# Two attention layers of a decoder: key tiles added up on GpSimd, projections in pieces, maxima three slots ahead

## The reference

```python
def _L1_attn_ref(x, w_q, w_k, w_v, w_o):          # x is layer-normalised
    q, k, v = x @ w_q.T, x @ w_k.T, x @ w_v.T     # 16 heads of 32
    scores = einsum('bhqd,bhkd->bhqk', q, k) / sqrt(32)
    return (softmax(scores) @ v) @ w_o.T
def _L1_xattn_ref(q, latent_kv, Wq, Wkv_expand, Wout):
    k, v = split(latent_kv @ Wkv_expand.T, 2)     # latent_kv has 128 columns
    scores = where(causal, (q @ Wq.T) k / sqrt(32), lowest)
    return (softmax(scores) @ v) @ Wout.T
x = x + _L1_attn_ref(layernorm(x), ...)
x = x + _L1_xattn_ref(layernorm(x), ctx_512, ...)
x = x + _L1_ffn_ref(layernorm(x), ...)            # "the network", which follows
```

## Time and profile before

| What | us |
|---|---|
| Median of three runs | 2957.02 |
| The profiled execution | 2967.87 |
| Its span | 2966.1 |
| Start of the self layer (its input is loaded) | 1494 |
| First scores with maxima (L440) | 1555.7 |
| Last sums (L463) | 2397.9 |
| First matmul of the network (L2691) | 2424.0 |

### The profile page before, as it was taken

The page is one execution under the profiler, slowest core; times in us unless marked ns, Lnnn a source line. Parts: engine busy times, 40 slices in busy tenths (PEclk is TensorE's granted clock), DMA queues, the critical chain, the costliest instruction groups (busy, mean ns, idle before and its releaser), DMA issues. The chain is left out here.

```text
span 2966.1 us, 34593 instructions
## 1 busy us (share of the span) xinstructions
PE 2490.3 (84%) x12822; PEld 1652.2 (56%) x12822; DVE 1781.1 (60%) x2772; ACT 1225.8 (41%) x1859; POOL 791.4 (27%) x1054
## 2 busy tenths in 40 slices
PE   5899999984344369889769999999999879999999
PEld 4554545421222248788645454545555548888887
DVE  3766666546799977777636655655565444444443
ACT  3343434335766725455314333443433223333332
POOL 2223232213566626878600000001211110000000
PEclk8999999986666679999879999999999889999999
DMA  3313132202222357999732323333533331101000
GB/s 108 77 44 86 44 86 47 68 19 94 85 94 90 111 186 221 268 255 268 188 95 65 93 72 78 91 97 94 128 88 94 115 125 67 43 1 43 1 29 15
DMA packets 177017, 287.09 MB, mean 97 GB/s; under 512 B 20769, under 2 KB 52385, under 8 KB 176866
## 3 DMA queue, kind: packets, MB, share of 16 engines
q1 hardware_dynamic: 159458, 249.73, 28.7%
q0 software_dynamic: 14336, 34.61, 5.4%
q10 hardware_dynamic: 3072, 0.79, 0.1%
HBM read 149.79 MB, written 58.98 MB: 70 GB/s over the span
## 5 line engine op out<-in xcount | busy, mean ns | idle before, releaser
L657 DVE TENSOR_REDUCE at_negmax<-at_ps 128x2 f32<-128x1024 f32 (+3 forms) x256 | 259.2, 1017 | 131.5 <-PE at_ps L420 66.6
L572 ACT ACTIVATE at_probs<-at_ps 128x1024 f32<-128x1024 f32 (+3 forms) x256 | 221.8, 866 | 265.3 <-PE at_ps L440 262.5
L1258 DVE TENSOR_REDUCE a_negmax<-a_ps 128x2 f32<-128x1024 f32 x128 | 155.2, 1217 | 137.4 <-PE a_ps L1011 136.8
L50 PE MATMUL ff_ps<-ff_xnT_hi,ff_s_hi 128*128 128x512 f32 x512 | 201.0, 393 | 5.1 <-DVE ff_xnT_lo L2782 5.1
L52 PE MATMUL ff_ps<-ff_xnT_hi,ff_s_lo 128*128 128x512 f32 x512 | 200.2, 391 | 0.0
L51 PE MATMUL ff_ps<-ff_xnT_lo,ff_s_hi 128*128 128x512 f32 x512 | 200.1, 391 | 0.0
L1842 ACT ACTIVATE gr_act_signs<-gr_signed,gr_test 128x512 bf16<-128x512 f32 x248 | 177.3, 717 | 25.6 <-POOL gr_test L2221 14.0
L1159 ACT ACTIVATE a_probs<-a_ps 128x1024 f32<-128x1024 f32 x128 | 130.9, 1024 | 137.8 <-PE a_ps L1029 137.3
L2812 DVE TENSOR_TENSOR ff_hid<-ff_hid,ff_ps 128x512 f32<-128x512 f32 x64 | 44.0, 688 | 238.8 <-ACT ff_hid L2757 238.8
L440 PE MATMUL at_ps<-at_qk 98*128 98x512 f32 (+3 forms) x512 | 171.7, 417 | 17.6 <-DMA at_qk<-at_mrow 10.8
L440 PEld LDWEIGHTS at_ps<-at_qk 98*128 98x128 f32 x512 | 83.1, 193 | 158.7 <-issue 89.9
(11 more groups left out here) (416 smaller groups left out, 6425.9 us busy)
## 6 DMA issues: line engine op xcount, KB each, us to landing
at_qk<-at_part SPq DMA_DIRECT2D x384, 128.0 KB, 2.3
first_gu<-in_L_ffn_w_gate_up_dram SPq DMA_DIRECT2D x32, 1024.0 KB, 6.2
a_qk<-a_part SPq DMA_DIRECT2D x192, 128.0 KB, 2.3
first_d<-in_L_ffn_w_down_dram SPq DMA_DIRECT2D x32, 512.0 KB, 7.8
gr_aside_raw<-in_L_ffn_W_dram SPq DMA_DIRECT2D x48, 256.0 KB, 3.3
w13T<-gr_aside_out SPq DMA_DIRECT2D x32, 256.0 KB, 3.2
shared_x<-x_after_cross SPq DMA_DIRECT2D x8, 1024.0 KB, 8.0
ff_slab<-w13T SPq DMA_DIRECT2D x14, 512.0 KB, 6.3
```

The lines of the kernel that those rows point to most:

```text
L50: pe.matmul(out, lh, rh, start=start, stop=False, skip_group_check=True)
L572: act.activation(probs[:, t % 2, 2 * w:2 * w + 2, lo:S], banks(("kq", g, s), lo), ACT.Exp, scale=SCALE).then_inc(free(("kq", g, s)), 1)
L657: dve.reduce_max(negmax[:, g % 2, :].rearrange("p (j t) -> p j t", t=NT)[:, 2 * w:2 * w + 2, t], banks(("qk", g, s), 0, width(g, t)), AX.X ...
L1258: dve.reduce_max(negmax[:, g % 2, :].rearrange("p (j t) -> p j t", t=NT)[:, 2 * w:2 * w + 2, t], banks(("qk", g, s)), AX.X, negate=True).t ...
```

## The change

*Sums.* The exponentials of a pair get a buffer of their own: five of them (`halves` and a third of `got`), three in turn for pair 0 and two for pair 1. GpSimd adds the second to fourth key tile of each pair onto the first (`fold`, six additions per step, at slots 2 to 7, 128 x 1024 numbers each in the self layer); the first of them waits until the first tile has been weighed. `add_up` runs once per group, in slot 1 of the next step, in a pair of banks that it takes in turn, and waits for all six additions. `weigh` stands at slots 2, 4, 6 and 0. An exponential waits for the addition and the weighing that free its buffer.

*Maxima ahead.* `scores_qk` and the reductions run three slots earlier (`ahead`); `turn_maxima` and both `maxima_rows` stand at slot 5 of the step before instead of at its end.

*Projections.* The 8 pieces of a projection (three matmuls each) stand in slots 1, 2, 3, 5, 6 and 7 (`PIECES`), with one bank, PROJ, which was that of the sums, for q and then for k; ScalarE and VectorE empty it at slot 4 and at the end of the step.

*Inputs.* The transposes stand at slot 0 of c = 1; the input is measured in step c = 3 of the batch before, and normalised on GpSimd, one tile each at slots 1 to 4 of c = 0.

*The network's second chunk* is loaded after the last store of the loop, since one of the five buffers lies in its place.

```diff
-        probs = sb("probs", [P, 2, QUAD, S])
+        halves = sb("halves", [P, 4, 2, S])
...
-        NUM, SUMS = 6, 7
+        NUM, PROJ = 6, 7
+        SHIFT, TURN, NORMALIZE = 3, 5, 6
+        PIECES = {1: (0,), 2: (1,), 3: (2, 3), 5: (4,), 6: (5,), 7: (6, 7)}
...
-        UNITS = {(1, 1): ("o", 0), (1, 4): ("o", 1), (1, 6): ("x", 0), (2, 3): ("v", 0), (3, 3): ("v", 1)}
+        UNITS = {(1, 1): ("o", 0), (1, 4): ("o", 1), (1, 0): ("x", 0), (2, 3): ("v", 0), (3, 3): ("v", 1)}
...
+        def ahead(g, s):
+            return divmod(PAIRS * (g + 1) + s + SHIFT, PAIRS)
...
+        def both_of(g, t, w):
+            i = ((0, 1, 2, 1)[t] - g) % 3 if w == 0 else 3 + (g + (t > 0)) % 2
+            return halves[:, i] if i < 4 else got[:, 2]
+
+        def probs_of(g, t, j):
+            return both_of(g, t, j // 2)[:, j % 2, :]
...
+                load_chunk(0)
+
+            def load_chunk(k):
+                sp.dma_start(ff_chunk(got, None, k)[:, 0:2, :], w13T.rearrange("(k p) (m e) -> k p m e", p=P, m=2)[k]).then_inc(ff_in, 16)
+                sp.dma_start(ff_chunk(got, None, k)[:, 2, :], w2_mixed.rearrange("(k p) d -> k p d", p=P)[k]).then_inc(ff_in, 16)
...
+            sp.wait_ge(sums_done, G)
+            sp.wait_ge(values_done, NT * G)
+            for k in range(1, FF_AHEAD):
+                load_chunk(k)
...
-            def add_up(g, t):
-                lo = first(g, t)
-                if t == 0 and g >= 1:
-                    pe.wait_ge(sums_out, g)
+            def add_up(g):
+                key = claim("s", g)
+                for w in range(2):
+                    pe.wait_ge(folded[w], (NT - 1) * (g + 1))
                 for j in range(QUAD):
-                    mm = pe.matmul(ps[j * HD:(j + 1) * HD, SUMS, lo:S], ones[:], probs[:, t % 2, j, lo:S],
-                                   start=t == 0, stop=t == NT - 1, skip_group_check=True)
+                    mm = pe.matmul(bank(key, 0)[j * HD:(j + 1) * HD, :], ones[:], probs_of(g, 0, j), start=True, stop=True, skip_group_check=True)
...
-            def project(g):
+            def project(g, piece):
                 c, b = g % NC, g // NC
-                wait_drained(pe, "xT", b, 1)
-                if cross(b):
-                    wait_drained(pe, "cT", b)
-                    wait_drained(pe, "w", 0)
-                    wait_drained(pe, "w", 1)
-                    if c >= 2:
-                        wait_drained(pe, "w", 2)
-                key = claim("p", g)
-                for i, (w, src, n) in enumerate(((wqT, xnT, NC), (cross_wkT, cT, 1) if cross(b) else (wkT, xnT, NC))):
-                    for dc in range(n):
-                        mm = split_mm(pe, bank(key, i), [p[:, dc, c * P:(c + 1) * P] for p in w], [p[:, dc, :] for p in src], dc == 0, dc == n - 1)
+                i, dc = piece // NC, piece % NC
...
+                    if 2 * g + i:
+                        pe.wait_ge(p_out, 2 * g + i)
...
+                mm = split_mm(pe, ps[:, PROJ, :], [p[:, dc, c * P:(c + 1) * P] for p in w], [p[:, dc, :] for p in src], dc == 0, dc == n - 1)
+                if dc == n - 1:
...
-                    if has(g + 1):
-                        scores_qk(g + 1, s)
-                    if s >= 2 and has(g):
-                        half(g, s - 2)
-                    if s < 2 and has(g - 1):
-                        half(g - 1, PAIRS - 2 + s)
+                    if has(ahead(g, s)[0]):
+                        scores_qk(*ahead(g, s))
+                    if s == TURN and has(g + 1):
+                        turn_maxima(g + 1)
+                    if s >= 2 and s % 2 == 0 and has(g):
+                        weigh(g, s // 2 - 1)
+                    if s == 0 and has(g - 1):
+                        weigh(g - 1, NT - 1)
+                    if s == 1 and has(g - 1):
+                        add_up(g - 1)
...
-                if has(g + 1):
-                    turn_maxima(g + 1)
-                if has(g + 3):
-                    project(g + 3)
+                    if has(g + 3):
+                        for piece in PIECES.get(s, ()):
+                            project(g + 3, piece)
...
-                if NT * g + t >= 2:
-                    act.wait_ge(sums_done, NT * g + t - 1)
-                act.activation(probs[:, t % 2, 2 * w:2 * w + 2, lo:S], banks(("kq", g, s), lo), ACT.Exp, scale=SCALE
+                if t == 0 and g:
+                    act.wait_ge(values_done, NT * g - (1, 0)[w])
+                    act.wait_ge(folded[w], (NT - 1) * g - (1, 0)[w])
+                if t == 1 and g:
+                    act.wait_ge(sums_done, g)
+                if t == 3 or (t, w) == (2, 1):
+                    old = t - 2 + w
+                    act.wait_ge(values_done, NT * g + old + 1)
+                    act.wait_ge(folded[w], (NT - 1) * g + old)
+                act.activation(both_of(g, t, w)[:, :, lo:S], banks(("kq", g, s), lo), ACT.Exp, scale=SCALE
...
+            def keep_projection(g, i):
+                if g and i == 0:
+                    act.wait_ge(stack_in[(g - 1) % STACKS], 16 * 3 * QUAD * ((g - 1) // STACKS + 1))
+                act.wait_ge(p_ready, 2 * g + i + 1)
+                act.copy(part[:, 1 + i, :], ps[:, PROJ, :]).then_inc(p_hi, 1)
...
-            def layernorm(b):
-                dve.wait_ge(rstd_done, b + 1)
-                for t in range(NT):
-                    dve.tensor_scalar(xs(b)[:, t, :], xs(b)[:, t, :], mv[:, t, 0:1], rstd[:, t:t + 1],
-                                      ALU.subtract, ALU.mult).then_inc(xn_done, 1)
...
+            def low_projection(g, i):
+                dve.wait_ge(p_hi, 2 * g + i + 1)
+                dve.tensor_tensor(part[:, 3 * i, :], ps[:, PROJ, :], part[:, 1 + i, :].bitcast(F32), ALU.subtract).then_inc(p_out, 1)
...
+            def fold(g, t, w):
+                lo = first(g, t)
+                if causal(g):
+                    pool.wait_ge(masked, PAIRS * (g - NC * B) + 2 * t + w + 1)
+                else:
+                    wait_drained(pool, "kq", g, 2 * t + w)
+                if t == 1:
+                    if not causal(g):
+                        wait_drained(pool, "kq", g, w)
+                    pool.wait_ge(values_done, NT * g + 1)
+                else:
+                    pool.wait_ge(folded[w], (NT - 1) * g + t - 1)
+                total, part_of = both_of(g, 0, w)[:, :, lo:S], both_of(g, t, w)[:, :, lo:S]
+                pool.tensor_tensor(total, total, part_of, ALU.add).then_inc(folded[w], 1)
...
+            def layernorm(b, t):
+                if t == 0:
+                    pool.wait_ge(rstd_done, b + 1)
+                pool.tensor_scalar(xs(b)[:, t, :], xs(b)[:, t, :], mv[:, t, 0:1], rstd[:, t:t + 1], ALU.subtract, ALU.mult).then_inc(xn_done, 1)
...
-                for s in range(PAIRS if has(g) and causal(g) else 0):
-                    mask_diagonal(g, s)
-                if has(g - 1):
-                    pool.wait_ge(rec_done, NT * g)
-                    if g - 1 >= NC:
-                        pool.wait_ge(y_ready, 2 * ((g - 1) // NC))
-                    pool.tensor_tensor(oT[:, (g - 1) % NC, :], weighed[:, 0, :], weighed[:, 1, :], ALU.mult).then_inc(o_done, 1)
-                if g % NC == 0 and 1 <= g // NC + 1 < ALL:
-                    rstds(g // NC + 1)
+                for s in range(PAIRS):
+                    if has(g) and causal(g):
+                        mask_diagonal(g, s)
+                    if has(g) and s >= 2:
+                        fold(g, s // 2, s % 2)
+                    if g % NC == 0 and 1 <= s < 1 + NT and 1 <= g // NC + 1 < ALL:
+                        layernorm(g // NC + 1, s - 1)
+                    if s == NORMALIZE and has(g - 1):
+                        normalize(g - 1)
```

99 lines of the change are left out of this document (55 added, 44 removed).

## The result

The changed kernel takes 2974.73 us (median of six runs, 2969.69 to 2986.30), the kernel before 2960.26 (six runs beside it): a ratio of 1.0057, with a 95% interval of 1.0033 to 1.0080. It is slower by some 15 us where 74 less were forecast. Its profiled execution has a span of 2970.6 us, 4.5 more than the one before.

A forecast was written before the change was run, and what follows sets the result against it. TensorE was taken to set the time, almost alone in the self layer. Self layer -53, cross layer -32, start +4 and network +7 gave -74 us, 2883 at the median (before: 2957); 8-in-10 range 2845 to 2925.

The forecast's parts named there:

- So they just fit, with nothing over: Self layer: GpSimd's six additions and normalising per group, 15.6 us, fit a bare group's 19.8 and end before the sums.
- the count of 11.7 us against some 17: Cross layer: GpSimd's additions, eight masks and normalising take 11.7 us per group, against a group of some 17.
- Masks behind the normalisings: Cross layer, first group of a batch: masks wait behind input normalisings, 1.3 us three times, 4 us lost.
- Normalising: Layer's input on GpSimd: 1.45 us per tile, at most 2.9; only late exponentials cost, 3 us; at 2.9, 30 us.
- The clock: Cross layer's end: TensorE ran at 0.70 of its clock for 45 us; fewer waits there gain 7 us.
- The sums in the self layer: Three of four quads of sums per group leave TensorE, 47.5 us saved.
- The end: Cross layer's last two groups: waits of 7.7 and 3.1 us become work, 11 us gained, 3 lost again.
- The start: First batch's start: nothing covers the normalisings and the turns of the single bank, 4 us net lost.
- the new wait for the rows of maxima: First score of each cross group: rows of maxima land 1.7 us late, 12 times, 20 us lost.
- GpSimd becomes the bound: Rival, chance 0.08: additions of 3.35 us and normalisings of 2.9 or more make GpSimd late, taking the whole gain: 2970.
- The cross layer gives nothing: Rival, chance 0.13: late stack transfers make waits of 3 to 4 us per group and lower TensorE's clock: 2916.
- GpSimd blocks VectorE: Rival, chance 0.04: VectorE's reciprocals wait half a GpSimd addition each, 4 x 1.2 us a group: 2907.

The follow-up runs named there:

- the normalisings in the gap: Changed kernel with all four normalisings of the layer's input on VectorE in slot 1 of a batch's first group, where GpSimd pauses: 2934 us, ratio 0.9906.
- masks first: Changed kernel with GpSimd making both masks of a key tile before that tile's two additions in the cross layer: 2955 us, ratio 0.9984.
- gap, early load, masks first: Changed kernel with the normalisings in the gap, the early load and masks first together: 2912 us, ratio 0.9823.
- narrow additions: Changed kernel with each of a group's six additions on 2 x 32 columns only, so the sums lack the rest: 2912 us, ratio 0.9848.
- gap, early load, masks first, narrow: The kernel of gap, early load, masks first with each addition on 2 x 32 columns only: 2895 us, ratio 0.9784.
- the two and the early load: Changed kernel with the normalisings in the gap, the cross layer's additions on VectorE one slot later, and the early load: 2936 us, ratio 0.9926.
- the run without masks: Changed kernel without the masks on the cross layer's diagonal blocks and the waits for them: 2947 us, ratio 0.9955.
- the early load: Changed kernel with the network's second chunk loaded ahead of the last two stores instead of behind them: 2970 us, ratio 1.0032.

## Why the prediction was wrong, point by point

**The step that failed** is "So they just fit, with nothing over", and for the cross layer the count of 11.7 us against some 17. Both compare GpSimd's busy time with the length of a group. What decides is which instruction stands behind which. It sets three prices wrong:

- *Masks behind the normalisings* were 4 us; the waits for masks are 31 us, because masks also stand behind additions, and in every group. The order alone gave 20 us back at the median, the normalisings in the gap 15 us of the cross layer.
- *Normalising*: 1.45 us taken, 2.08 measured, inside the bounds. The last addition was followed to the sums, where it is late by some 1 us per wait (8.8 us in the layer). The late exponential behind it, put at "about 0.7 us on a bank", costs up to 2.9 us at the scores, four times, and 1.1 more behind (14.8 us in the layer, where 3 were counted), with a low clock after it. By the stretches of the run with the gap the normalisings cost 39 us, where the upper bound of 2.9 us each had been put at 30.
- *The clock* was to gain 7 us in the cross layer. It cost about as much as the added waits. The stretch from group 16 to the last sums, by busy time and by the sum of TensorE's waits in the order of time:

| Kernel | stretch | waits | TensorE busy | granted clock |
|---|---|---|---|---|
| before (2221 matmuls) | 380.8 | 30.5 | 349.7 | 0.95 |
| changed (1831) | 399.1 | 52.2 | 345.9 | 0.88 |
| masks first (1831) | 375.7 | 43.0 | 331.6 | 0.92 |
| gap, early load, masks first (1830) | 374.3 | 38.9 | 334.3 | 0.91 |
| narrow additions (1831) | 363.8 | 34.7 | 328.3 | 0.94 |
| gap, early load, masks first, narrow (1831) | 356.4 | 30.5 | 324.8 | 0.95 |

The same 1831 matmuls take 324.8 us at 0.95 and 345.9 at 0.88, 21 us more, while the waits grew by 22 from the kernel before. At the old clock the sums that went were worth 349.7 - 324.8 = 25 us, for 28 in the forecast; in the changed kernel 4 of it are left. That the waits bring the clock down is argued and not shown: clock and waits go together over most of the table, and the rows above show a slow stretch behind a wait twice, but no run changed one without the other, and a run outside the table doesn't fit (the two and the early load: 40.5 us of waits, 353.8 busy, 0.86).

**Right terms.** The sums in the self layer: the stretch is 19.0 us shorter while TensorE's idle time in it rose from 14.0 to 37.9 us, so its busy time fell by 43, for 47.5. The addition's 2.38 us. The wait for the last maximum. The end: the last two groups before the last take 49.3 us for 58.3, 9 less (8 forecast), but that holds their share of the sums too, and the last group gives 6.4 back to masks. The start, 5.5 for 4, from the normalisings: it is 66.9 to 71.0 us in the runs with these on GpSimd and 60.5 to 63.1 in those without. The load behind the last store, 4.9 for 7, and its remedy 5.5.

**A wrong term that didn't decide:** the new wait for the rows of maxima, 20 us. It is 3.8 us in the cross layer. In the run without masks it is 10.7, so other waits may hide part of it; with narrow additions and all remedies it is 4.8, so the projections and scores of slots 5 to 7 cover most of it after all.

**The rivals.** "GpSimd becomes the bound", 0.08, comes nearest. Its place was right (first groups of a batch, masks waiting with it) and its point wrong: it was to decide from 3.3 us for an addition, and the loss came at 2.39 and 2.08. That its 2970 lies near the time is partly luck, since it had the sums 70 us late, which were 8.8 late in the self layer; exponentials, masks and the clock made up for it. "The cross layer gives nothing", for late stacks, had the effect (low clock behind waits of 1 to 5 us) with another cause. "GpSimd blocks VectorE" doesn't happen in the changed kernel, where VectorE's reciprocals and statistics keep their 0.94 and 0.64 us; the runs that put such an instruction there show it.

**The signs.** Those listed as right mostly came: no long wait at the turn, additions of 2.39 us, GpSimd busy 63% of the self layer, groups without units every 21.5 us, the network 7.2 us behind the last store (8 or more were asked). Of those listed as wrong only the waits at the sums came, just (8.8 us in four batches). None asked for masks or exponentials, where most of the loss was.

**What stays open.** With the additions narrow and the three remedies, the stage is 68.7 us shorter than before, for 92 that the forecast's terms give without the charges then gone (load 7, start 4, exponentials 3, masks 4). Of these 23 us, 11 are in the self layer and 12 in the cross layer. Their busy times tell where (columns as above; each time the kernel before, the changed one, and the one with narrow additions and all remedies, in the self layer and then from group 16 to the last sums):

```profile
1555.65:2017.12 461.47, 447.44 (x2254) 235.01 (x2254) 268.54 (x338) 183.33 (x210) 23.68 (x21) 1.00 0.33 84
...
1557.06:1999.52 442.46, 404.60 (x1875) 232.54 (x1876) 257.66 (x322) 181.90 (x210) 277.12 (x131) 0.98 0.34 87
...
1545.52:1961.30 415.78, 399.62 (x1876) 229.59 (x1876) 263.52 (x338) 182.21 (x210) 52.03 (x116) 0.99 0.36 93
```

```profile
2017.12:2397.93 380.81, 349.67 (x2220) 209.85 (x2221) 208.15 (x310) 134.08 (x205) 74.48 (x147) 0.95 0.36 97
...
1999.52:2398.63 399.11, 345.91 (x1830) 216.15 (x1831) 197.06 (x291) 137.17 (x206) 225.20 (x258) 0.88 0.34 90
...
1961.30:2317.74 356.44, 324.77 (x1831) 202.56 (x1831) 202.21 (x303) 135.98 (x206) 102.34 (x245) 0.95 0.38 101
```

In the self layer the sums' work went in full in the last of these, 47.8 us for 47.5, but TensorE's idle time (the stretch less its busy time) is 16 us for the 14 before: the 9 us of waits at the turn came back as other short ones, for banks and inputs. In the cross layer the idle time is the same, 32 us for 31, and the work fell by 25, where 28 of sums and 7 of clock were counted. What causes each of the short waits no run took apart. Nor is it settled why second groups of the self layer take 37.0 us at a clock of 1.00 in some runs and 38.6 at 0.96 in others, with the same program for that layer: in two that were compared the waits of TensorE are alike, the longest 1.0 us, and one has a stretch at the lower clock level behind them and the other has none.

## What to carry to other kernels

An idle engine has room for work only behind what it already does for others: before moving work there, write its queue down in order and ask for each instruction that someone waits for what stands ahead of it. Sums of busy time can fit while short, urgent instructions (a mask, an addition that frees a buffer) are each late by one long one. Then put the urgent ones first, and give a long one to an engine that is free when the queue pauses: with the early load, which was worth 5 us, that took 62 us off here, four times the loss.

## What the runs showed of the hardware

- On GpSimd one tensor and two scalar pointers cost more per column than the sum of two tensors: 2.08 us for 128 x 512 against 2.39 for 128 x 1024, 4.1 ns a column against 2.3. Lengths alone, as in the forecast's two bounds, didn't order its instructions here.
- VectorE's normalising (one tensor input, 0.55 us) waited for a GpSimd addition that ran, up to 2.7 us in all; an addition of two tensors took 1.88 us beside GpSimd (1.22 for a multiplication alone), and GpSimd's went from 2.39 to 2.56. Statistics (0.64 us) and reciprocals (0.94) kept their time.
- In both places shown, a wait of TensorE of 2.9 and 4.7 us was followed by matmuls at half the clock (granted clock 0.50): a weighing's matmul at 1.07 us for 0.62, a score pair at 1.16 for 0.73.
